# Four transformer layers on one core: the last norm turned by token halves, and another head order in the second attention's first group

## The chip, the cores and the metric

The kernel runs on one core of a Trainium2 chip. The metric is the device time of one launch in microseconds (us). The kernel before was run three times on the chip; a further execution was taken with the hardware profiler.

## What is computed

The input x has 2 batches of 256 tokens and 512 features, 512 tokens in all; the context has 2 batches of 512 tokens. Four layers follow one another. Each one adds an attention block on the normed x to x, and then a feed-forward block on the normed x. Two of these eight blocks matter here.

The second attention (layer 1 of the reference, "l1" in the kernel) has 16 query heads of 96 features and 4 key and value heads, so 4 query heads share one of the latter. Its keys are the 512 context tokens and the 256 tokens of x itself:

```python
hidden = jnp.concatenate([context, latents], axis=1)
q = (latents @ Wq.T).reshape(b, q_len, H, HD)        # H = 16, HD = 96
scores = jnp.einsum('bkgqd,bksd->bkgqs', q, k) * scale
attn = jax.nn.softmax(scores, axis=-1)
```

The last feed-forward block (layer 3) looks at its own normed input before it multiplies: a feature whose largest magnitude over all 512 tokens is above 3 is an outlier.

```python
col_max = jnp.max(jnp.abs(x), axis=tuple(range(x.ndim - 1)))
outlier = col_max > THRESHOLD                        # 3.0
y = _ste_quant_rows(jnp.where(outlier, 0.0, x)) @ _ste_quant_rows(W).T
y = y + jnp.where(outlier, x, 0.0) @ W.T + b
```

So no product with the outliers can start before the largest magnitude of that feature over both token halves is known.

## The kernel before, in words

Every engine has its own hand-ordered program, and semaphores join them. TensorE does all products, nearly all as three passes of a high and a low part (`passes`, L337 to L341). ScalarE (ACT) writes high parts, VectorE (DVE) low parts, GpSimd (POOL) splits the weights, and the queue of SyncE (SP) issues every DMA, one after the other in program order.

**Attention.** The class `Attention` (from L729) works in slots. A group of 4 heads and 2 batches has 16 tiles of 128 queries, one for each slot k; two tiles are a unit (one head of one batch, 256 queries). In slot k TensorE computes the scores of tile k (`scores`, L1190), DVE the row maximum (`largest`, L1306), ACT the exponential; one slot later ACT and DVE write the two fp16 parts of the probabilities (L1258, L1360), and SP issues the DMA that transposes them (`cross_probs`, L1100). The scores go round two banks, so tile k waits for the DVE part of tile k-2 (L1209). At slot 2u+5 TensorE multiplies unit u with the values (`attend`, L1221), which have come through a transposing DMA too (`cross_values`, L1108); ACT and DVE then write its two output planes over the unit's queries (L1298, L1394), which DVE signals by `s_olo`. Projections of the next group's queries, keys and values and of the last group's output are dealt out to the slots by lists (`FIRST`, `MIDDLE`, `LAST`, L587 to L602).

**The packed fourth head of l1.** A head has 96 rows, so the projection makes three tiles of 128 rows: heads 0, 1 and 2 with 32 rows of head 3 below each. Six DMAs, two for each tile, assemble head 3 (`move_queries`, L864, `s_qmove`); in the first group they are issued at slots 1 and 2, between the transposes. For the same reason the output of head 3 is spread back under the three others by six DMAs for each batch (`move_out`, L872), before the output projection: for the first batch at slot 10 of the group, for the second at slot 2 of the next. `move_out` waits for `s_olo`. The order in which the units take the heads is `head` (L833): 0, 1, 3, 2 in all four groups of l1. Head 3 so is the third unit (tiles 4 and 5), and `move_out` waits for three units of its batch.

In l1 the queue of SP also loads rows of the last block's weights, one DMA in each slot from 8 to 39 (`RowMaxima`, L605): DVE takes the row maxima two slots later (L630).

**The last norm.** `Norm` 7 (L399) turns the normed x so that features lie on partitions. DVE adds the last output tile to x, takes the statistics, and waits for the inverse deviation from POOL (L463); the first two token tiles were normed before, so TensorE turns them while the third and fourth are still being made. Each of the four banks holds one block of 128 features with all 512 tokens (L499 to L506), so a bank is full only when the fourth token tile has been turned. Then ACT copies it to `xF` (L2209), DVE takes the largest magnitudes (L2221) and the masks (L2222, L2223), ACT writes the high part of the outliers (L2206) and DVE the low part (L2217), feature block by feature block. TensorE starts the first product (`out_first`, L2240) block by block as the low parts come. ACT and DVE next take the largest magnitude of each token (L2320, L2400), which TensorE turns after the second output tile (L2231). POOL splits the next weights meanwhile (L2178, L2180). Norms 1, 3 and 5 already turn by halves of 256 tokens, with a bank for two feature blocks of one half (L487 to L498).

## Time and profile before

| | |
|---|---|
| runs of the kernel | 1871.99, 1865.81, 1871.82 us; median 1871.82 us |
| the profiled execution, its own time | 1868.25 us |
| its span, first to last instruction | 1866.5 us |
| TensorE busy | 1746.1 us (94% of the span) |
| VectorE busy | 1427.1 us (76%) |
| ScalarE busy | 1048.1 us (56%) |
| GpSimd busy | 886.5 us (47%) |
| mean granted TensorE clock | 0.981 of full speed |

The span leaves 1.75 us of the profiled execution's time outside. All times of the trace are from the span's start. An engine's busy time says how much it had to do; where it waited and for whom stands in the views by waits and in the timelines. PE is the matmul side of TensorE, SPq the DMA queue that SyncE drives. A granted clock of 1.00 in a stretch is the level of 2.4 GHz, 0.50 that of 1.2 GHz.

### The profile page before, as it was taken

How to read it: one execution, taken by the hardware profiler on the slowest of the kernel's cores; microseconds unless marked ns; L12 is line 12 of the kernel's file. 1: busy time of each engine (PE TensorE's matmuls, PEld its weight loads, DVE VectorE, ACT ScalarE, POOL GpSimd, SP SyncE). 2: the span in 40 equal slices, each digit the busy share in tenths (PEclk: the TensorE clock that was granted, in tenths of full speed). 3: DMA queues.
4: the chain of work that ended last, by engine and by line, in shares of the span. 5: the costliest groups of instructions: out<-in, count | busy, mean ns of one | idle time of the engine just before them, and what ended most of it. 6: DMA issues, size and time to landing. Idle time of an engine off the chain costs nothing.

```text
span 1866.5 us, 29004 instructions
## 1 busy us (share of the span) xinstructions
PE 1746.1 (94%) x9916; PEld 1417.3 (76%) x9916; DVE 1427.1 (76%) x3036; ACT 1048.1 (56%) x1999; POOL 886.5 (47%) x863
## 2 busy tenths in 40 slices
PE   6999999999888999979899999999989999998988
PEld 5777777787677788868788888888867778776755
DVE  6877888878777887756777778778864687787898
ACT  5766677667126555632656556556641487776233
POOL 6876776774732222053434444343347541333752
PEclk9999999999999999989999999999999999998998
DMA  5666656566418988761788878979762100120110
GB/s 183 139 115 147 138 117 142 132 116 123 118 29 167 208 194 168 145 132 57 136 164 182 156 161 182 172 159 200 137 142 104 51 15 10 48 90 29 68 45 23
DMA packets 524177, 226.13 MB, mean 121 GB/s; under 512 B 493696, under 2 KB 503168, under 8 KB 516736
## 3 DMA queue, kind: packets, MB, share of 16 engines
q1 hardware_dynamic: 524032, 224.28, 55.6%
q8 instruction: 81, 1.33, 0.3%
q14 instruction: 64, 0.52, 0.1%
HBM read 97.08 MB, written 5.24 MB: 55 GB/s over the span
## 4 chain that ended last, share of the span: by engine, by line
PE 66%; DVE 18%; ACT 5%; DMA 4%; issue 4%; POOL 2%; SPq 2%; DVEq 0%; POOLq 0%; ACTq 0%
PE ps_t L339 9%; PE ps_t L340 8%; PE ps_t L341 8%; PE ps_s L339 7%; PE ps_s L341 7%; PE ps_s L340 7%; PE ps_o L339 3%; PE ps_o L340 3%; PE ps_o L341 3%; PE ps_o L1961 3%; PE ps_t L1992 3%; ACT ps_s L1285 2%; PE ps_s L1947 2%; DVE l_q_lo L1035 2%; DVE l_ab L1360 2%
## 5 line engine op out<-in xcount | busy, mean ns | idle before, releaser
L1285 ACT ACTIVATE ps_s<-ps_s,nmax 128x768 f32<-128x768 f32 (+1 forms) x320 | 252.4, 789 | 326.7 <-DVE nmax L1315 242.5
L1258 ACT ACTIVATE l_ab<-ps_s,rinv 128x768 f16<-128x768 f32 (+1 forms) x320 | 260.6, 814 | 80.6 <-DVE rinv L1370 58.0
L1360 DVE SCALAR_TENSOR_TENSOR l_ab<-ps_s,rinv,l_ab 128x768 f16<-128x768 f32 (+1 forms) x320 | 288.9, 903 | 4.4 <-ACT l_ab L1258 4.0
L1315 DVE TENSOR_REDUCE nmax<-ps_s 128x1 f32<-128x768 f32 x192 | 183.4, 955 | 125.0 <-PE ps_s L341 124.4
L339 PE MATMUL ps_o<-l_pt,l_v 128*128 128x256 f16 (+1 forms) x832 | 231.3, 278 | 14.0 <-DMA l_pt<-l_ab 6.4
L341 PE MATMUL ps_o<-l_pt,l_v 128*128 128x256 f16 (+1 forms) x832 | 230.0, 276 | 0.0
L340 PE MATMUL ps_o<-l_pt,l_v 128*128 128x256 f16 (+1 forms) x832 | 229.9, 276 | 0.0
L339 PE MATMUL ps_s<-l_k_hi,l_q_hi 128*128 128x512 f32 (+3 forms) x512 | 187.0, 365 | 25.6 <-DVE l_ab L1360 20.7
L377 POOL TENSOR_TENSOR wo_hi<-raw_big,one 128x512 fp32r<-128x512 f32 (+2 forms) x100 | 102.8, 1028 | 201.7 <-PE ps_t L341 123.3
L340 PE MATMUL ps_s<-l_k_lo,l_q_hi 128*128 128x512 f32 (+3 forms) x512 | 180.3, 352 | 0.0
L341 PE MATMUL ps_s<-l_k_hi,l_q_lo 128*128 128x512 f32 (+3 forms) x512 | 180.0, 352 | 0.0
L377 POOL TENSOR_TENSOR wq_hi<-raw_big,one 128x512 fp32r<-128x512 f32 (+1 forms) x100 | 102.2, 1022 | 137.2 <-DMA raw_big<-in_l_wq 64.6
L339 PEld LDWEIGHTS ps_s<-l_k_hi,l_q_hi 128*128 128x128 f32 (+1 forms) x512 | 96.9, 189 | 64.7 <-DVE l_ab L1360 33.6
L379 POOL TENSOR_TENSOR wq_lo<-raw_big,wq_hi 128x512 fp32r<-128x512 f32 (+1 forms) x100 | 129.0, 1290 | 7.8
L716 POOL TENSOR_TENSOR w_raw<-w_raw,w_row 128x512 f32<-128x512 f32 x32 | 41.4, 1293 | 188.0 <-DMA w_raw<-in_f_w 188.0
L379 POOL TENSOR_TENSOR wo_lo<-raw_big,wo_hi 128x512 fp32r<-128x512 f32 (+2 forms) x100 | 121.3, 1213 | 7.8
L2100 DVE TENSOR_TENSOR l_pt_lo<-ps_t,l_pt_hi 128x512 fp32r<-128x512 f32 x128 | 88.4, 691 | 46.8 <-ACT l_pt_hi L2034 43.9
L339 PE MATMUL ps_t<-xT_hi,wq_hi 128*128 128x512 f32 (+1 forms) x296 | 117.5, 397 | 4.3 <-DVE xT_lo L2217 3.1
L339 PEld LDWEIGHTS ps_o<-l_pt,l_v 128*128 128x128 f16 (+1 forms) x832 | 87.4, 105 | 43.1 <-issue 29.9
L1312 DVE CUSTOM_DVE_ANT_0 ps_s<-ps_s,l_mask 128x512 f32<-128x512 f32 x128 | 88.6, 692 | 40.8 <-PE ps_s L341 40.6
L340 PE MATMUL ps_t<-xT_lo,wq_hi 128*128 128x512 f32 (+1 forms) x296 | 111.2, 376 | 0.0
L341 PE MATMUL ps_t<-xT_hi,wq_lo 128*128 128x512 f32 (+1 forms) x296 | 110.9, 375 | 0.0
(390 smaller groups left out, 4949.3 us busy)
## 6 DMA issues: line engine op xcount, KB each, us to landing
raw_big<-in_l_wq SPq DMA_DIRECT2D x18, 1024.0 KB, 5.7
raw_big<-in_l_wo SPq DMA_DIRECT2D x18, 1024.0 KB, 6.0
w_raw<-in_f_w SPq DMA_DIRECT2D x32, 256.0 KB, 3.5
raw_big<-in_f_w SPq DMA_DIRECT2D x7, 1024.0 KB, 4.8
raw_kv<-in_l_wkv SPq DMA_DIRECT2D x12, 512.0 KB, 6.6
l_pt<-l_ab SPq DMA_TRANSPOSE x320, 3.7
raw_f<-in_f_w SPq DMA_DIRECT2D x4, 1024.0 KB, 4.7
w_nat<-in_f_w1n SPq DMA_DIRECT2D x16, 256.0 KB, 3.8
```

The source lines that it names most:

```text
L339: pe.matmul(o, a[0], b[0], start=start, stop=False)
L340: pe.matmul(o, a[0], b[1], start=False, stop=False)
L341: return pe.matmul(o, a[1], b[0], start=False, stop=stop)
L377: pool.tensor_tensor(hi, w, one[0:parts, 0:1].to_broadcast([parts, cols]), ALU.mult).then_inc(w_rdy[role], 1)
L379: pool.tensor_tensor(lo, w, hi.bitcast(F32), ALU.subtract).then_inc(w_rdy[role], 1)
L1258: e.activation(sp.ab[:, (k - 1) % 3, 0, :], self.scores_out(k - 1), ACT.Copy, scale=rinv[:, i:i + 1]).then_inc(s_pa, 1)
L1285: e.activation(self.scores_out(k), self.scores_out(k), ACT.Exp, bias=nmax[:, i:i + 1], scale=-1.0 if l.rope else 1.0, accum_out=rsum[:, i: ...
L1312: e.tensor_tensor_reduce(out=o, in0=o, in1=sp.mask[:, 2 * b + qt, :], scale=-1.0, scalar=F32_MAX, op0=ALU.add, op1=ALU.min, accum_out=nmax ...
L1315: e.tensor_reduce(nmax[:, i:i + 1], o, AX.X, ALU.max, negate=True).then_inc(s_max, 1)
L1360: e.scalar_tensor_tensor(out=b, in0=self.scores_out(t), scalar=rinv[:, i:i + 1], in1=a, op0=ALU.mult, op1=ALU.subtract).then_inc(s_pb, 1)
L1961: mm = e.matmul(ps_o[:, 0:SQ], l3v[blk % 2][:, k, g * P:(g + 1) * P], l3pt[u % 2][y][:, k, :], start=g == 0 and k == 0 and y == 0, stop=g ...
L2100: e.tensor_tensor(pt[1], ps_t[p % 2][:, :].rearrange("p (k q) -> p k q", q=P), pt[0].bitcast(F32), ALU.subtract).then_inc(s3["tlo"], 1)
```

## The change

The first part concerns the last norm. TensorE turns it as norms 1, 3 and 5: the first two token tiles fill two banks, each with two feature blocks of 256 tokens, and the last two fill the other two. ACT copies a bank as soon as it is full, so the first half's two before the second half is normed. The new helper `f3_norm_largest` takes the largest magnitudes of one bank (two feature blocks, 256 tokens). DVE calls it for the first half's banks after the statistics and before it norms the second half, and for the second half's afterwards. A small new instruction takes the larger of the two halves' values, and the masks are made for two feature blocks at once. The new tile `q_cm_halves` holds the values of the halves.

The second part concerns l1. In its first group (its first 8 units) the heads come in the order 0, 1, 2, 3; the other groups keep 0, 1, 3, 2. `move_out` of the first group therefore waits for four units of its batch and not for three.

```diff
--- before.py
+++ after.py
@@ -206,6 +206,7 @@
         q_cm = at("q_cm", [P, HT], F32, 61.5625)
         q_mo = at("q_mo", [P, HT], F32, 61.625)
         q_mi = at("q_mi", [P, HT], F32, 61.6875)
+        q_cmh = at("q_cm_halves", [P, 2, DK], F32, 61.84375)
         q_tm = at("q_tm", [P, TT], F32, 61.75)
         q_ts = at("q_ts", [P, TT], F32, 61.78125)
         h = at("h", [P, HT, T], F32, R0)
@@ -428,6 +429,8 @@
                 if self.halves:
                     self.dve_stats(e, link, 1)
                     if self.i == 7:
+                        f3_norm_largest(e, 0)
+                        f3_norm_largest(e, 1)
                         self.dve_scale(e, 1)
                         f3_norm_dve(e, link)
                         return
@@ -484,7 +487,7 @@
                 return self.banks[2 * half + p].rearrange("p (d t) -> p d t", d=2)
 
             def pe(self, e, early=None):
-                if self.halves and self.i != 7:
+                if self.halves:
                     for t in range(TT):
                         half = t // 2
                         e.wait_ge(s_xn, TT * self.i + t + 1)
@@ -493,16 +496,8 @@
                                              xn[:, t, d * P:(d + 1) * P], ident[:, :])
                             if t % 2 and d % 2:
                                 mm.then_inc(g_full, 1)
-                        if t == 1:
+                        if t == 1 and early is not None:
                             early(e)
-                    return
-                if self.halves:
-                    for t in range(TT):
-                        e.wait_ge(s_xn, TT * self.i + t + 1)
-                        for d in range(DK):
-                            mm = e.transpose(self.banks[d][:, t * P:(t + 1) * P], xn[:, t, d * P:(d + 1) * P], ident[:, :])
-                            if t == TT - 1:
-                                mm.then_inc(g_full, 1)
                     return
                 e.wait_ge(s_xn, TT * (self.i + 1))
                 if self.i == 0:
@@ -832,7 +827,7 @@
 
             def head(self, u):
 
-                return (0, 1, 3, 2)[u % HG] if self.l.packed else u % HG
+                return (0, 1, 3, 2)[u % HG] if self.l.packed and u >= UNITS else u % HG
 
             def o_planes(self, u, hd):
                 hh, b = self.head(u), u // HG % B
@@ -873,7 +868,7 @@
 
                 cols = slice(b * SQ, (b + 1) * SQ)
                 e.wait_ge(s_qmove, 96 * (g + 1))
-                e.wait_ge(s_olo, self.c.unit + g * UNITS + b * HG + 3)
+                e.wait_ge(s_olo, self.c.unit + g * UNITS + b * HG + (3 if g else 4))
                 for a in self.s.q[g % 2]:
                     for t in range(3):
                         e.dma_start(a[96:P, t, cols].bitcast(F32), a[32 * t:32 * t + 32, 3, cols].bitcast(F32)).then_inc(s_omove[b], 16)
@@ -1190,7 +1185,7 @@
                 def scores(k):
                     g, i = k // TILES, k % TILES
                     u, qt = i // 2, i % 2
-                    b, hh = u // HG, self.head(u)
+                    b, hh = u // HG, self.head(g * UNITS + u)
                     if b == 0 and qt == 0:
                         if hh < l.qt:
                             self.operand_ready(e, self.find["q", g, hh, False])
@@ -2202,28 +2197,40 @@
 
         def f3_norm_act(e):
             def hi(d):
-                e.wait_ge(s4["x_mask"], 2 * d + 2)
+                e.wait_ge(s4["x_mask"], 2 * (d // 2) + 2)
                 e.activation(xT[0][:, d, :], xF[:, d, :], ACT.Copy, scale=q_mo[:, d:d + 1]).then_inc(g_hi, 1)
+            for n in range(4):
+                half, p = n // 2, n % 2
+                e.wait_ge(g_full, cf.g - 4 + n + 1)
+                e.activation(xF[:, 2 * p:2 * p + 2, half * SQ:(half + 1) * SQ], norms[7].half_bank(half, p), ACT.Copy)\
+                    .then_inc(s4["x_kept"], 1)
             for d in range(DK):
-                e.wait_ge(g_full, cf.g - 4 + d + 1)
-                e.activation(xF[:, d, :], last_norm_banks[d], ACT.Copy).then_inc(s4["x_kept"], 1)
-                if d:
-                    hi(d - 1)
-            hi(DK - 1)
+                hi(d)
+
+        def f3_norm_largest(e, n):
+            half, p = n // 2, n % 2
+            e.wait_ge(s4["x_kept"], n + 1)
+            return e.tensor_reduce(q_cmh[:, half, 2 * p:2 * p + 2], xF[:, 2 * p:2 * p + 2, half * SQ:(half + 1) * SQ], AX.X, ALU.max,
+                                   apply_absolute_value=True)
 
         def f3_norm_dve(e, link):
             def lo(d):
                 e.wait_ge(g_hi, START["ln7"].hi + d + 1)
                 e.scalar_tensor_tensor(out=xT[1][:, d, :], in0=xF[:, d, :], scalar=q_mo[:, d:d + 1],
                                        in1=xT[0][:, d, :].bitcast(F32), op0=ALU.mult, op1=ALU.subtract).then_inc(g_free, 1)
-            for d in range(DK):
-                e.wait_ge(s4["x_kept"], d + 1)
-                link(e.tensor_reduce(q_cm[:, d:d + 1], xF[:, d, :], AX.X, ALU.max, apply_absolute_value=True))
-                e.tensor_scalar(q_mo[:, d:d + 1], q_cm[:, d:d + 1], 3.0, None, ALU.is_gt).then_inc(s4["x_mask"], 1)
-                e.tensor_scalar(q_mi[:, d:d + 1], q_cm[:, d:d + 1], 3.0, None, ALU.is_le).then_inc(s4["x_mask"], 1)
-                if d:
-                    lo(d - 1)
-            lo(DK - 1)
+
+            def masks(p):
+                two = slice(2 * p, 2 * p + 2)
+                link(e.tensor_tensor(q_cm[:, two], q_cmh[:, 0, two], q_cmh[:, 1, two], ALU.max))
+                e.tensor_scalar(q_mo[:, two], q_cm[:, two], 3.0, None, ALU.is_gt).then_inc(s4["x_mask"], 1)
+                e.tensor_scalar(q_mi[:, two], q_cm[:, two], 3.0, None, ALU.is_le).then_inc(s4["x_mask"], 1)
+            link(f3_norm_largest(e, 2))
+            masks(0)
+            link(f3_norm_largest(e, 3))
+            lo(0)
+            masks(1)
+            for d in range(1, DK):
+                lo(d)
 
         def f3_pe(e):
             def turn_largest(o):
```

## Rows read from the trace of the kernel before

**Rows 1.** The page: busy time of the engines, share of the span.
```profile
PE 1746.1 (94%) x9916; PEld 1417.3 (76%) x9916; DVE 1427.1 (76%) x3036; ACT 1048.1 (56%) x1999; POOL 886.5 (47%) x863
```
**Rows 2.** The page: the chain that ended last, shares of the span.
```profile
PE 66%; DVE 18%; ACT 5%; DMA 4%; issue 4%; POOL 2%; SPq 2%; DVEq 0%; POOLq 0%; ACTq 0%
```
**Rows 3.** Timeline of TensorE, first group of l1: start, us, instruction, idle before, releaser.
```profile
565.82 0.49 PE L339 MATMUL ps_s<-l_k_hi,l_q_hi 96*128 96x512 f32 x1 [3.87 <-DMA l_q_lo<-l_q_lo]
...
571.47 0.41 PE L339 MATMUL ps_o<-l_pt,l_v 128*96 128x256 f16 x1
...
574.35 0.48 PE L339 MATMUL ps_s<-l_k_hi,l_q_hi 96*128 96x512 f32 x1
```
**Rows 4.** Timeline of VectorE in the same stretch.
```profile
562.47 1.00 DVE L1360 SCALAR_TENSOR_TENSOR l_ab<-ps_s,rinv,l_ab 128x768 f16<-128x768 f32 x1
...
567.44 0.96 DVE L1315 TENSOR_REDUCE nmax<-ps_s 128x1 f32<-128x768 f32 x1 [2.57 <-PE ps_s L341]
...
575.69 0.96 DVE L1315 TENSOR_REDUCE nmax<-ps_s 128x1 f32<-128x768 f32 x1
```
**Rows 5.** Busy time by stretch: PE, PEld, DVE, ACT, POOL; then granted clock, DMA.
```profile
562.00:566.00 4.00, 0.18 (x1) 0.18 (x2) 2.70 (x5) 2.74 (x5) 0.00 (x0) 1.00 0.81 160
566.00:570.00 4.00, 3.30 (x14) 2.74 (x15) 2.39 (x5) 1.15 (x3) 0.00 (x0) 0.59 0.84 157
...
624.00:628.00 4.00, 2.82 (x15) 2.10 (x14) 3.21 (x7) 1.51 (x3) 0.00 (x0) 1.00 1.06 163
```
**Rows 6.** Timeline of SP's queue, slots 4 to 17 of l1.
```profile
565.82 1.83 SPq L1113 DMA_TRANSPOSE l_v<-l_vab  x1
...
594.25 0.85 SPq L622 DMA_DIRECT2D w_nat<-in_f_w1n  x1
595.20 1.80 SPq L879 DMA_DIRECT2D l_q_hi<-l_q_hi  x3
...
598.99 1.44 SPq L1105 DMA_TRANSPOSE l_pt<-l_ab  x1
...
625.48 0.58 SPq L622 DMA_DIRECT2D w_nat<-in_f_w1n  x1
```
**Rows 7.** The line of `cross_values` (L1113) from 560 to 570 us: its landing.
```profile
DMA to landing us min/median/max: 3.8/3.8/3.8
```
**Rows 8.** Timeline of VectorE, slots 11 to 18 of l1.
```profile
597.21 0.47 DVE L1394 SCALAR_TENSOR_TENSOR l_q_lo<-ps_o,v_out_scale,l_q_hi 96x256 fp32r<-96x256 f32 x1
...
605.83 0.67 DVE L630 TENSOR_REDUCE q_sw<-w_nat 128x1 f32<-128x512 f32 x1
...
619.33 0.69 DVE L630 TENSOR_REDUCE q_sw<-w_nat 128x1 f32<-128x512 f32 x1 [0.52 <-DMA w_nat<-in_f_w1n]
...
628.89 0.69 DVE L630 TENSOR_REDUCE q_sw<-w_nat 128x1 f32<-128x512 f32 x1 [1.50 <-DMA w_nat<-in_f_w1n]
```
**Rows 9.** The first `attend` of the third attention: timeline of TensorE.
```profile
902.03 0.39 PE L339 MATMUL ps_o<-l_pt,l_v 128*128 128x256 f16 x1 [2.76 <-DMA l_v<-l_vab]
```
**Rows 10.** Busy time by stretch after it, columns as in Rows 5.
```profile
902.00:906.00 4.00, 3.96 (x19) 2.85 (x20) 0.01 (x1) 0.00 (x0) 2.14 (x2) 0.50 0.71 151
```
**Rows 11.** Timeline of all engines in the last norm.
```profile
1715.73 1.00 DVE L418 TENSOR_SCALAR xn<-x,mv,rstd 128x512 f32<-128x512 f32 x2 [0.81 <-POOL rstd L463]
...
1717.25 1.08 ACT L2209 ACTIVATE xF<-ps_s 128x512 f32<-128x512 f32 x2 [10.76 <-PE ps_s L503]
...
1717.88 0.69 DVE L2221 TENSOR_REDUCE q_cm<-xF 128x1 f32<-128x512 f32 x1 [1.15 <-ACT xF L2209]
...
1720.88 0.76 PE L339 MATMUL ps_t<-xT_hi,wq_hi 128*128 128x512 f32 x1 [3.12 <-DVE xT_lo L2217]
...
1725.67 0.79 PE L339 MATMUL ps_t<-xT_hi,wq_hi 128*128 128x512 f32 x1
...
1730.26 0.66 PE L2231 MATMUL ps_s<-ident,q_amx 128*128 128x128 f32 x4 [0.20 <-DVE q_amx L2400]
```
**Rows 12.** The line of the low parts (L2217): duration in ns, least, median, largest.
```profile
L2217 DVE SCALAR_TENSOR_TENSOR xT_lo<-xF,q_mo,xT_hi x4: 741/1030/1562, 1719.6 to 1724.1; 128x512 fp32r<-128x512 f32 x4
```

## The prediction

> **What bounds the kernel now.** I read the page first: TensorE is busy for 94% of the span [rows 1] and has 66% of the chain that ended last, VectorE 18% [rows 2]. So a gain must shorten a stretch in which TensorE waits or runs at a low clock, and must not be given back by a later wait. The change touches two such stretches, which I read in the timelines.
>
> *Start of the second attention (l1).* The scores of tile 4, the first that need the assembled head 3, start at 565.82 after 3.87 us of idle time, released by the last of the moving DMAs [rows 3]. Their other condition, the probabilities of tile 2, was met at 562.47 + 1.00 = 563.5 [rows 4]. So head 3 costs 2.3 us there. Behind it the clock falls: TensorE has 0.18 us of work in 562 to 566, and from 566 to 570 the granted clock is 0.59, against 1.00 before [rows 5]. It is the level of 1.2 GHz for most of the time up to about 573.5; the first unit's products with the values, 571.47 to 574.35, run mostly in it, and so last 2.9 us [rows 3].
>
> *Slots 10 to 16 of the same group.* The queue of SP issues without a gap from the row DMA at 594.25 to the one at 625.48 (31 issues from the first up to the last; none begins over 0.12 us after the end of the one ahead) [rows 6]. Its last one releases VectorE at 628.89 after a wait of 1.50 us, an earlier one at 619.33 after 0.52 us [rows 8]. TensorE, full before, has 2.82 of 4 us in 624 to 628 [rows 5]. So at 628.89 it is SP's queue that sets the time of all engines; what they gain before it is lost there unless SP starts earlier too.
>
> *The last norm.* VectorE waits 0.81 us for the inverse deviation, norms the second half at 1715.73, ACT copies from 1717.25, the first maximum starts at 1717.88 and the first product at 1720.88; its last block starts at 1725.67 [rows 11]. The next thing that TensorE waits for is the turned token maxima, at 1730.26 with 0.20 us of wait [rows 11].
>
> **Part 1, the head order.** Nothing is added or removed: the same 12 moving DMAs, the same matmuls. Moved are the uses of head 3 (tiles 4, 5 to tiles 6, 7) and the condition of `move_out`.
>
> *The ramp.* Tile 4 starts at 563.5 in place of 565.8. Tile 5 then follows at about 566.9, a period of 3.4 us as between the tiles ahead. Its scores end at 568.3. Now the first unit's product with the values is next, and that needs the transposed values: issued at 565.82 behind the same DMAs as before, landed 3.8 us later, at 569.6 [rows 6, 7]. It was no wait before; now it is one of 1.3 us or a little more. If the clock is full, the product takes some 2 us in place of 2.9 (estimate: the part up to 573.5 halved), and tile 6 starts at 572.0 in place of 574.35 [rows 3]: a gain of 2.3 us. If the clock falls at this new wait, the product takes 3.9 us, tile 6 starts at 573.8 and its own scores take 1.2 us longer, so the maximum of tile 6, at 575.69 before [rows 4], comes 0.6 us later. For that stands the same spot of the third attention, which has no moved head: there the first product with the values waits 2.76 us for just this transfer [rows 9], and the clock of the 4 us behind is 0.50 [rows 10]. Ends: +2.3 and -0.6 us. I take 1.3: the new wait is half as long as that one, and work lies on both sides of it.
>
> *The hold at slot 10.* `move_out` of the first batch waited for unit 2; now it waits for unit 3, whose low part is written at 597.21 + 0.47 = 597.7 [rows 8]. SP was free for it at 595.1 [rows 6]. Behind it in the queue stand the transpose of tile 10 (598.99) and everything to 625.48 [rows 6]. Relative to the engines SP stops for 2.6 us. If the engines are d earlier, the queue starts 2.6 - d later than before, and since it runs without a gap, so does the issue at 625.48 and the release at 628.89. The rows between take part of the loss ahead of time (the row of 605.83 had about 1.7 us to spare, that of 619.33 none [rows 8]), but not twice. So part 1 is worth 2.6 - d, not -d: with d = 1.3 it costs 1.3 us; ends 0.3 and 3.2. The second batch's `move_out` waits for unit 7, which is done about when SP comes to it: nothing. The DMAs of slot 13 and 15, queries and weights of the next groups, come late with the queue; they had slots to spare.
>
> **Part 2, the norm.** The two maxima of the first half are 0.69 us each [rows 11], 1.38 us in a wait of 0.81: the second half is normed 0.57 us later. POOL's power runs beside them, so I put its cost at nothing; if they slowed it, that would cost its excess in full. A bank is full after the second block, not the first: 0.1 us. So VectorE's first maximum behind it starts at 1718.55. One maximum 0.69, the larger of two and the masks 0.45 (estimate from the small instructions around, 0.15 each), one high part 0.7 on ACT with the second maximum beside it, one low part 1.1 to 1721.5; masks 0.45; three low parts at 1.03 to 1.1 [rows 12] to 1725.2. Before, four maxima and four pairs of masks stood between the low parts, to 1725.6. So VectorE gains 0.4 us; with all three at 0.74 or at 1.56 [rows 12] it would be a gain of 1.4 or a loss of 1.0. TensorE starts at 1721.5 in place of 1720.88, but without gaps: twelve passes of 512 columns at 1.2 GHz are 5.1 us (estimate), to 1726.6, before 1727.1. Half of that half microsecond counts, since the clock returns no earlier, and the 0.20 us of wait may go. I take -0.2 us; ends -0.7 and +0.9. The early ACT copies cost nothing: ACT idles there. POOL's weight split begins 0.57 us later and is wanted some 9 us after its end.
>
> **Sum.** 1.3 - 0.2 = +1.1 us. On the profiled execution's 1868.25 us that is 1869.4. The median of the runs shown is 1871.82, 3.6 us above that execution, with one run at 1865.81; I take the middle of execution and median, 1870.0, as the base: **1871.1 us**.
>
> **The rivals.** *Faster: the ramp's gain is kept.* SP's queue turns out elastic: its transposes took 1.4 to 2.9 us each, and after a pause they may take the shorter time. Then d = 2.3 stays and the norm's 0.2 to 0.7 comes on top: 1867.3 us. Against it stands the release at 628.89, straight from the queue.
>
> *Slower: the clock falls at the first product with the values, and the hold is paid in full.* Place: 568 to 577 us. Price: 0.6 us at tile 6 and 2.6 at the hold, less 0.2: +3.0, 1873.0 us. It decides once the wait for the values grows from the 1.3 us of my sum towards the 2.76 of [rows 9]; a transfer slower by 1 us, as tile 3's transpose is now issued right behind it, would do.
>
> *Slower in the norm: the low parts come one after another.* They took up to 1.56 us, the longest without a maximum in front [rows 12]. If each is stopped by a weight split of POOL, three of them end at 1726.6, TensorE starts its last block 0.9 us late, and the norm costs 0.7 instead of gaining 0.2: 1872.0 us. The Trainium skill's page "SBUF — State Buffer", section "SBUF: two separate sides", says that a VectorE instruction with two SBUF inputs and a GpSimd one that reads SBUF hold a shared port as an exclusive lock, and "Who interferes with whom" there says that a reduction never contends; by that rule the reductions leave the interval between the low parts and only contending work is left, as in this rival. The spread of [rows 12] agrees with a lock, but its median of 1.03 does not show every one stopped.
>
> *The change doesn't do what it says:* the maxima of the first half do not fit in the wait (1.38 against 0.81 us), which my sum has; if they also come late, because ACT's copies do, up to 0.6 us more.
>
> **How the numbers follow.** Forecast 0.45; gain kept 0.17; clock and hold 0.20; norm's low parts 0.12; the rest 0.06. Base and changes: the best is -2.3 - 0.7 on the lowest run, 1863; the worst +3.2 + 0.9 on 1872, and a longer half-clock stretch of up to 2 us, 1878. Range 1863 to 1878. A change of 0.5% is 9.3 us, about what a measurement of this kernel can tell from none; no case reaches it. I leave 0.03 for faster and 0.04 for slower, 0.93 for the same.
>
> **What would show it.** TensorE's wait for the moved query should be gone and one for the transposed values stand before the first product with the values; `move_out` should start at the low part of unit 3 with SP idle ahead of it; VectorE should wait longer in total for the weight rows up to slot 18. In the norm the wait for the inverse deviation is gone, the first product starts about 0.6 us later and its last block 0.4 us earlier. I am wrong if SP's queue has gaps between slots 11 and 16, if the stretch from the start of l1 to the end of its first group is over 2 us shorter, or if the norm changes by over 1 us.

## The result, and the profile after

The changed kernel takes 1874.76 us (median of 17 runs, 1867.77 to 1880.21), the kernel before, run beside it, 1867.72 us (17 runs, 1859.52 to 1874.33). The ratio is 1.0038, with a 95% interval of 1.0026 to 1.0051: 7.1 us slower, 4.9 to 9.5 by the interval. A later measurement of both gave 1.0016 (1.0000 to 1.0032), that is 3.0 us. The first says slower, by 0.3 to 0.5%; the second's interval reaches down to no difference. A value of about 5 us lies in both intervals. The profiled execution took 1878.34 us with a span of 1876.5. Two of the 12 executions of the run with the heads alone, below, were slow (2621.55 and 6008.47 us) and are left out of its ratio, though not of its median.

**The page after.** TensorE's busy time is 6.1 us up on [rows 1], VectorE's 5.3; VectorE's share of the chain that ended last went from 18% [rows 2] to 20%.

```profile
PE 1752.2 (93%) x9908; PEld 1425.0 (76%) x9916; DVE 1432.4 (76%) x3034; ACT 1048.9 (56%) x1999; POOL 885.3 (47%) x863
...
PE 66%; DVE 20%; ACT 5%; issue 3%; DMA 3%; POOL 2%; SPq 1%; DVEq 0%; POOLq 0%; ACTq 0%
```

**The last norm after.** VectorE's timeline: start, us, instruction, idle time before it and what ended it. It answers to [rows 11, 12].

```profile
1722.14 0.17 DVE L414 TENSOR_SCALAR veps<-mv 128x2 f32<-128x2 f32 x1
1722.21 1.27 DVE L2213 TENSOR_REDUCE q_cm_halves<-xF 128x2 f32<-128x512 f32 x2
1723.40 0.99 DVE L419 TENSOR_SCALAR xn<-x,mv,rstd 128x512 f32<-128x512 f32 x2
1726.20 0.69 DVE L2213 TENSOR_REDUCE q_cm_halves<-xF 128x2 f32<-128x512 f32 x1 [1.80 <-ACT xF L2205]
1726.92 0.95 DVE L2224 TENSOR_TENSOR q_cm<-q_cm_halves 128x2 f32<-128x2 f32 x1
1727.91 0.17 DVE L2225 TENSOR_SCALAR q_mo<-q_cm 128x2 f32<-128x2 f32 x1
1727.98 1.24 DVE L2226 TENSOR_SCALAR q_mi<-q_cm 128x2 f32<-128x2 f32 x1
1729.14 0.67 DVE L2213 TENSOR_REDUCE q_cm_halves<-xF 128x2 f32<-128x512 f32 x1
1730.08 0.75 DVE L2219 SCALAR_TENSOR_TENSOR xT_lo<-xF,q_mo,xT_hi 128x512 fp32r<-128x512 f32 x1 [0.27 <-ACT xT_hi L2201]
1730.75 1.23 DVE L2224 TENSOR_TENSOR q_cm<-q_cm_halves 128x2 f32<-128x2 f32 x1
1732.02 0.97 DVE L2225 TENSOR_SCALAR q_mo<-q_cm 128x2 f32<-128x2 f32 x1
1732.90 0.16 DVE L2226 TENSOR_SCALAR q_mi<-q_cm 128x2 f32<-128x2 f32 x1
1732.97 3.09 DVE L2219 SCALAR_TENSOR_TENSOR xT_lo<-xF,q_mo,xT_hi 128x512 fp32r<-128x512 f32 x3
```

Two numbers per partition are compared in each of the small instructions, and four of six take 0.95 to 1.24 us where the prediction had 0.15 each. Beside them GpSimd splits the second weight chunk without a gap (its timeline):

```profile
1724.48 1.04 POOL L2173 TENSOR_TENSOR wo_hi<-raw_big,one 128x512 fp32r<-128x512 f32 x1 [1.39 <-DVE xn L419]
1725.59 1.26 POOL L2175 TENSOR_TENSOR wo_lo<-raw_big,wo_hi 128x512 fp32r<-128x512 f32 x1
1726.82 1.04 POOL L2173 TENSOR_TENSOR wo_hi<-raw_big,one 128x512 fp32r<-128x512 f32 x1
1727.94 1.26 POOL L2175 TENSOR_TENSOR wo_lo<-raw_big,wo_hi 128x512 fp32r<-128x512 f32 x1
1729.16 1.04 POOL L2173 TENSOR_TENSOR wo_hi<-raw_big,one 128x512 fp32r<-128x512 f32 x1
```

The slow comparisons end where a split ends: the one from 1727.98 ends at 1729.22, the split at 1729.20. TensorE waits for what comes of them (its timeline), and its clock is at the lower level of 1.2 GHz meanwhile (busy time by stretch, columns as in [rows 5]):

```profile
1730.98 0.76 PE L340 MATMUL ps_t<-xT_hi,wq_hi 128*128 128x512 f32 x1 [5.02 <-DVE xT_lo L2219]
1733.76 0.79 PE L340 MATMUL ps_t<-xT_hi,wq_hi 128*128 128x512 f32 x1 [1.17 <-DVE xT_lo L2219]
```

```profile
1726.00:1731.00 5.00, 0.02 (x1) 0.05 (x1) 4.46 (x7) 1.99 (x4) 4.84 (x5) 0.50 0.70 262
1731.00:1741.00 10.00, 8.79 (x21) 5.99 (x22) 8.28 (x12) 4.47 (x7) 3.77 (x3) 0.54 0.29 105
```

To compare kernels whose stages start at different times I count from veps, the instruction that adds 1e-5 to the second half's variance (1714.75 in before, 1722.14 here). The first product starts at 8.84 instead of 6.13, the copy of the fourth output tile by ACT at 25.89 instead of 21.69. From there on the tiles keep their distance of 4.2 us to the end of the 16 tiles (66.76 against 62.56). The count from veps to the end of the span says what the norm's part is worth to the whole kernel: in the five profiles of all runs that keep the norm of before it is 150.2 to 151.7 us (mean 150.9), in the four with the norm of the change 154.2 to 154.5 (mean 154.3), so 3.4 us.

**The start of l1 after.** TensorE's timeline, SP's queue, and TensorE again near slot 15; they answer to [rows 3], [rows 6] and [rows 8].

```profile
570.83 0.45 PE L340 MATMUL ps_o<-l_pt,l_v 128*96 128x256 f16 x1 [2.25 <-DMA l_v<-l_vab]
...
621.16 0.28 PE L340 MATMUL ps_o<-l_pt,l_v 128*96 128x256 f16 x1 [0.75 <-issue]
```

```profile
595.09 0.83 SPq L617 DMA_DIRECT2D w_nat<-in_f_w1n  x1
598.75 1.80 SPq L874 DMA_DIRECT2D l_q_hi<-l_q_hi  x3
600.59 1.85 SPq L874 DMA_DIRECT2D l_q_lo<-l_q_lo  x3
602.54 2.42 SPq L1100 DMA_TRANSPOSE l_pt<-l_ab  x1
```

```profile
570.00:574.00 4.00, 3.17 (x15) 3.02 (x16) 0.82 (x3) 0.60 (x2) 0.00 (x0) 0.50 1.06 198
```

The wait for the moved head is gone, a wait of 2.25 us for the transposed values has taken its place, and the clock in the 4 us behind it is 0.50. SP's queue stands idle for 2.8 us (595.92 to 598.75) before the moves, and the transpose of slot 10 behind them is issued at 602.54 instead of 598.99.

### The profile page after: what moved, and what is told of

Same layout as the page of the kernel before. It is cut to its first block, busy times and chain, and to the rows that moved or that the text cites. A ratio compares the mean times of both kernels' runs of the same rounds, so it can differ in the third digit from the quotient of the medians.

```text
span 1876.5 us, 28995 instructions
## 1 busy us (share of the span) xinstructions
PE 1752.2 (93%) x9908; PEld 1425.0 (76%) x9916; DVE 1432.4 (76%) x3034; ACT 1048.9 (56%) x1999; POOL 885.3 (47%) x863
## 4 chain that ended last, share of the span: by engine, by line
PE 66%; DVE 20%; ACT 5%; issue 3%; DMA 3%; POOL 2%; SPq 1%; DVEq 0%; POOLq 0%; ACTq 0%
PE ps_t L340 9%; PE ps_t L341 8%; PE ps_t L342 8%; PE ps_s L340 7%; PE ps_s L342 7%; PE ps_s L341 7%; PE ps_o L340 3%; PE ps_o L1956 3%; PE ps_o L341 3%; PE ps_o L342 3%; PE ps_t L1987 3%; ACT ps_s L1280 2%; PE ps_s L1942 2%; DVE nmax L1310 2%; DVE l_q_lo L1030 2%
```

## The experiments

Each run has its own time and that of before, taken in turns on the same chip; the difference is worked out from the ratio of the two (1.0021 is 3.9 us). The median of before was 1866.85 to 1868.46 us in these measurements.

| run | median us, runs | ratio to before (95%) | first high part | last low part ends | fourth tile |
|---|---|---|---|---|---|
| before | 1867.72, 17 | 1 | 4.10 | 10.86 | 21.69 |
| the change | 1874.76, 17 | 1.0038 (1.0026 to 1.0051) | 7.12 | 13.92 | 25.89 |
| the change again | 1870.81, 12 | 1.0016 (1.0000 to 1.0032) | 7.12 | 13.92 | 25.94 |
| norm alone | 1872.64, 12 | 1.0021 (1.0004 to 1.0037) | 5.85 | 13.76 | 25.23 |
| heads alone | 1871.47, 12 | 1.0022 (1.0002 to 1.0041) | 4.09 | 10.87 | 21.68 |
| norm, fused on one column | 1867.85, 12 | 1.0007 (0.9987 to 1.0028) | 5.16 | 12.20 | 22.30 |
| norm, splits behind the masks | 1870.83, 12 | 1.0011 (0.9988 to 1.0035) | 5.26 | 10.97 | 25.06 |
| norm, one column, tensor_tensor kept | 1871.75, 10 | 1.0023 (1.0007 to 1.0039) | 5.02 | 13.75 | 25.24 |
| norm, fused, one maximum ahead | 1866.23, 12 | 0.9995 (0.9979 to 1.0010) | 4.88 | 11.91 | 22.01 |

The last three columns are us behind veps, from the profile of each.

**The two parts by themselves.** The first run leaves out the head order, the second the norm's part.

```diff
-                return (0, 1, 3, 2)[u % HG] if self.l.packed and u >= UNITS else u % HG
+                return (0, 1, 3, 2)[u % HG] if self.l.packed else u % HG
-                e.wait_ge(s_olo, self.c.unit + g * UNITS + b * HG + (3 if g else 4))
+                e.wait_ge(s_olo, self.c.unit + g * UNITS + b * HG + 3)
```

> Only the last norm's part of the change; heads in the order of before. Theory (both parts cost, the norm's by its small VectorE instructions standing in GpSimd's weight splits): first high part about 7.1 us behind veps (4.1 in before), first product of the final stage about 8.8 us behind veps (6.1), time +3 to +4.5 us over before. Rival A (the head order makes all of the 7 us): 0 +- 1 us. Rival B (the norm makes all, the heads' loss is absorbed by the end): +6 to +7.5 us.

> Only the head order with its later moves; the last norm as before. Theory: the second attention's cross part ends about 3 us later (the wait for v, the clock at its lower level behind it, the SP queue held about 3 us), time +2 to +4 us. Rival A (the head order makes all): +6 to +7.5 us. Rival B (absorbed later on): 0 +- 1 us.

Measured +3.9 (0.7 to 6.9) and +4.1 us (0.4 to 7.7). Either part costs, if only just beyond its interval, and the sum of 8 agrees with the 7.1 of the whole. The intervals are too wide to put a rival with all the cost in one part out by the times alone; the positions can: the norm's part alone moves the fourth tile by 3.5 us, the heads alone by nothing (21.68). The first high part came at 5.85 and the first product at 7.76, earlier than the 7.1 and 8.8 expected from the change's profile: there the third copy by ACT starts 3.43 us behind veps, here 2.79, so some 0.6 us of the change's 4.2 are not its small instructions.

**What stops the small instructions.** In the first of three runs no two-column instruction and no tensor_tensor is left among the masks: the other half's maximum comes in as the scalar.

```diff
-                link(e.tensor_tensor(q_cm[:, two], q_cmh[:, 0, two], q_cmh[:, 1, two], ALU.max))
-                e.tensor_scalar(q_mo[:, two], q_cm[:, two], 3.0, None, ALU.is_gt).then_inc(s4["x_mask"], 1)
+                for d in (2 * p, 2 * p + 1):
+                    one_d = slice(d, d + 1)
+                    e.tensor_scalar(q_mo[:, one_d], q_cmh[:, 0, one_d], q_cmh[:, 1, one_d], 3.0, ALU.max, ALU.is_gt).then_inc(s4["x_mask"], 1)
```

> The norm's part alone, but the larger of the two halves and the comparison are one instruction on one column (128x1) with the other half as its scalar, so no two-column instruction and no tensor_tensor is left among the masks. Theory (two-column and two-input instructions are stopped by GpSimd's splits, one-column ones are not, as in before): each small one 0.14 to 0.20 us, first high part 4.2 to 4.8 us behind veps, time -1 to +1 us against before and 2.5 to 4 us under the norm's part alone. Rival (the order of the turns and the copies costs, not the small instructions): still +3 us or more.

```profile
1718.84 0.21 DVE L2225 TENSOR_SCALAR q_mo<-q_cm_halves 128x1 f32<-128x1 f32 x1
1718.97 0.20 DVE L2226 TENSOR_SCALAR q_mi<-q_cm_halves 128x1 f32<-128x1 f32 x1
...
1720.04 1.61 DVE L2219 SCALAR_TENSOR_TENSOR xT_lo<-xF,q_mo,xT_hi 128x512 fp32r<-128x512 f32 x1
```

None of the eight is stopped (0.20 to 0.22 us), the low part of 128x512 beside them is (1.61 us). The fourth tile is back from 25.2 to 22.3, and from veps to the end of the span it is 151.1 us instead of 154.1. The time is +1.3 us (-2.4 to +5.2), which by itself is not told apart from the norm's part alone. The first high part, at 5.16, missed the expected 4.2 to 4.8. The second run keeps the change's own instructions and holds GpSimd back until the masks stand:

```diff
                     e.wait_ge(s3["job_full"], L3_JOBS)
+                    e.wait_ge(s4["x_mask"], 4)
```

> The norm's part alone as the change has it, but GpSimd's splits of the second weight chunk wait until the last mask stands. Theory (GpSimd's instructions stop the small ones): two-column masks and the larger of the halves 0.15 to 0.25 us each without GpSimd beside them, first high part under 5 us behind veps, first product about 6 us behind veps, time -1 to +1 us. Rival (they are slow of themselves, about 1 us each): no change to the norm's part alone, +3 us.

```profile
1719.12 0.16 DVE L2225 TENSOR_TENSOR q_cm<-q_cm_halves 128x2 f32<-128x2 f32 x1
1719.32 0.17 DVE L2226 TENSOR_SCALAR q_mo<-q_cm 128x2 f32<-128x2 f32 x1
1719.39 0.17 DVE L2227 TENSOR_SCALAR q_mi<-q_cm 128x2 f32<-128x2 f32 x1
```

The same six instructions take 0.15 to 0.17 us without GpSimd beside them, so they are not slow of themselves. The expected positions were missed all the same: the first high part came at 5.26 us (under 5 expected), the first product at 6.98 (about 6), and the first tile at 12.08 is no gain, since the five profiles with the norm of before have it at 11.98 to 12.67. And the splits now fell on the four tensor_tensor of the tokens' largest magnitude (5.54 us in all), for which TensorE waits behind the second tile: third tile at 22.33 against 18.97, time +2.1 us (-2.2 to +6.5), where -1 to +1 was expected. The third run separates two inputs from two columns:

```diff
+                    link(e.tensor_tensor(q_cm[:, one_d], q_cmh[:, 0, one_d], q_cmh[:, 1, one_d], ALU.max))
+                    e.tensor_scalar(q_mo[:, one_d], q_cm[:, one_d], 3.0, None, ALU.is_gt).then_inc(s4["x_mask"], 1)
```

> The norm's part alone with everything small on one column, but the larger of the halves by tensor_tensor (two inputs in SBUF) and the comparisons by themselves, to part the two kinds of instruction. If both kinds are stopped by GpSimd's splits for their own reasons (two inputs; two columns): the four tensor_tensor of 128x1 take 0.5 to 1.3 us each where GpSimd runs, the eight comparisons 0.14 to 0.17 us, time +2 to +4 us. If only two-column instructions are stopped: all 0.15 to 0.2 us, time +0 to +1.5 us. If GpSimd stops whatever comes: comparisons of 0.5 us and more among them.

```profile
1716.42 0.60 DVE L2225 TENSOR_TENSOR q_cm<-q_cm_halves 128x1 f32<-128x1 f32 x1
1717.05 0.15 DVE L2226 TENSOR_SCALAR q_mo<-q_cm 128x1 f32<-128x1 f32 x1
1717.12 0.14 DVE L2227 TENSOR_SCALAR q_mi<-q_cm 128x1 f32<-128x1 f32 x1
1717.18 0.83 DVE L2225 TENSOR_TENSOR q_cm<-q_cm_halves 128x1 f32<-128x1 f32 x1
```

The first of the three outcomes, its time too (+4.3 us, 1.3 to 7.3): the four tensor_tensor of one number per partition take 0.60 to 1.18 us, the comparisons of one column 0.14 to 0.15. With the norm alone, two of the four comparisons of two columns took 0.97 and 1.25 us. So there are two separate reasons to be stopped: two inputs in SBUF, down to one number per partition, and a comparison of two columns. The Trainium skill's page "SBUF — State Buffer", section "Who interferes with whom", names both: two SBUF inputs against a GpSimd instruction that reads SBUF, and a mode that reads one tensor through both ports. The Trainium skill's page "VectorE: DVE Perf Modes", section "Mode 2×_2P — use both read ports for one tensor", wants for that mode that the outermost dimension larger than one is even, or odd and equal in source and destination. These runs agree with both pages: 128x2 has such a dimension and was stopped (up to 1.25 us), 128x1 has none and was not (0.14 to 0.15).

**One maximum ahead of the rows.** As the fused kernel, with the second maximum of the first half behind the normalised rows.

```diff
-                        f3_norm_largest(e, 1)
                         self.dve_scale(e, 1)
+                        f3_norm_largest(e, 1)
```

> The norm's part with one-column comparisons, and only one of the first half's two maxima ahead of the normalised rows, the other behind them, where VectorE idled 1.8 us. Theory (two maxima of 1.27 us do not fit into the wait of 0.81 us; one of 0.69 us does): xn 0.98 us behind veps as in before instead of 1.26, first product and the tiles of the final stage 0.3 us earlier than with one-column comparisons alone, time -1 to +0.5 us against before. Rival: another term (the copies' order, the clock) sets the start, tiles as with one-column comparisons alone within 0.1 us, +0.5 us.

The rows start 0.98 us behind veps (1.26 before that edit), every tile comes 0.28 us earlier than with the fused kernel. As expected; the time of -0.9 us (-3.9 to +1.9) against before is no measurable gain.

**The moves of the fourth head.** Three runs have SP's queue in another way. In the first two the heads stand in the order 0 to 3 as in the change, the norm as in before, and the first batch's moves are issued at slot 12 or 11 instead of 10; the third is before with nothing but the longer wait.

```diff
-                if s == 10:
+                if s == (10 if g else 12):
```

> The head order alone (last norm as before), with the first batch's moves of the fourth head issued two slots later, so that the SP queue finds the fourth unit done. Theory (the order's cost is the hold of the SP queue and the clock at the wait for v): no idle time of the queue between slots 9 and 10's transposes, the transposes of slot 10 on about 3 us earlier than with the head order alone, the cross part's slots 20 on at +1 to +2 us instead of +3, time +0 to +2.5 us over before, 1.5 to 3 us under the head order alone. Rival (the hold is hidden by the rounding's slack, all the cost is the clock at v): as the head order alone, +3 to +4 us.

> The head order alone, the first batch's moves of the fourth head issued one slot later (two slots later they only stood in front of the weight loads and the transpose of slot 13 was as late as with the hold). Theory (what costs is that the SP queue's run of moves and weight loads, which lasts until slot 15, is begun 3 us late): the moves find the fourth unit done and fill idle time of the queue, the transposes of slots 13 to 15 less than 1.5 us later than in before (counted from the stage's start), no wait of TensorE for a probability transpose near slot 15, time +0 to +2 us, what the clock at v leaves. Rival (the hold isn't what costs): as the head order alone, +3 to +4 us.

> Before with one edit: the moves of the first group wait for the fourth unit of their batch instead of the third; heads in the order 0, 1, 3, 2, last norm as before. Theory: the SP queue is held 2.5 to 3.5 us at slot 10, the slots from 20 on are 1.5 to 3 us later, time +1.5 to +3 us. Rival (the hold is hidden): 0 +- 1 us, slots from 20 on within 0.5 us of before.

Measured +3.0 (-0.2 to +6.2), +2.1 (-1.1 to +5.2) and +5.6 us (+2.6 to +8.8). The intervals of the first two hold the expected times and their rivals' alike; the third lies above the +1.5 to +3 expected. SP's queue in the run with slot 11, and its waits from 590 to 610 us (in total, times, longest):

```profile
595.50 0.90 SPq L622 DMA_DIRECT2D w_nat<-in_f_w1n  x1
597.65 1.42 SPq L1105 DMA_TRANSPOSE l_pt<-l_ab  x1
599.12 0.88 SPq L622 DMA_DIRECT2D w_nat<-in_f_w1n  x1
600.10 1.80 SPq L879 DMA_DIRECT2D l_q_hi<-l_q_hi  x3
601.94 2.69 SPq L879 DMA_DIRECT2D l_q_lo<-l_q_lo  x3
604.73 1.47 SPq L1105 DMA_TRANSPOSE l_pt<-l_ab  x1
```

```profile
SPq L1105 <- DVE l_ab L1360: 3.0, 3, 1.2
```

No idle time is left ahead of the moves there, but the queue is not busy throughout: with the moves out of the way it comes to the transposes before their probabilities are written, and waits for them three times, 3.0 us in total (596.40 to 597.65 is one). Before has no wait of the queue from 590 to 608 us; the change has 3.1 us from 590 to 610, nearly all ahead of the moves. Counted in every profile from 39.5 to 63 us behind slot 0, the queue waits 0.3 to 2.1 us for probabilities or for the moves' unit where the moves stand as in before, 2.3 to 3.0 with slot 11, 3.6 with slot 12, and 2.8 to 3.5 with the hold. Single executions wander by some us with the stretches of low clock, so I read a shorter distance, in the same way in every profile: between the row maxima (nmax) of two slots of l1, by the kernel's own slot numbers (slot 0 at 550.84 in before).

| kernels | profiles | slot 0 to 6 | 16 to 24 | 0 to 38 |
|---|---|---|---|---|
| order 0, 1, 3, 2, moves as in before | 10 | 25.5 (23.7 to 26.8) | 36.8 (35.3 to 37.9) | 162.1 (159.8 to 164.0) |
| order 0 to 3, moves held at slot 10 | 4 | 25.0 (24.0 to 25.6) | 38.9 (38.3 to 39.7) | 163.9 (162.8 to 164.7) |
| order 0 to 3, moves at slot 11 | 3 | 24.9 (23.9 to 25.6) | 39.6 (39.0 to 40.9) | 164.7 (164.3 to 165.0) |
| order 0 to 3, moves at slot 12 | 1 | 24.2 | 39.7 | 163.7 |
| hold alone | 1 | 24.7 | 38.8 | 163.9 |

(Mean, least and largest.) The order gains about 0.5 us on the mean by slot 6, less than the profiles differ among themselves. The stretch of slots 16 to 24 separates the groups: not one of the nine kernels with later moves is as short as the longest of the ten others. So the hold costs about 2.1 us there and 1.8 by the end of the cross part, where the ranges overlap, and the run with the hold alone shows the same by itself (its time, +5.6, is more than its slots account for; the rest was not found).

The clock enters this table. In slots 16 to 24 the granted clock is 1.00 throughout in seven of the ten profiles (mean 36.4 us), in the hold alone and in three of the four held ones (38.7); it has a stretch of the lower level, mean 0.955 to 0.958, in the three others of the ten (37.7), in the change (39.7) and in all with slot 11 or 12. At like clock the hold costs 2.2 and 2.0 us, slot 11 costs 1.3, 1.4 and 3.2, and slot 12 costs 2.0.

Moving the moves so did not give the time back, but it is no proof against the idle time as the cause either, since the queue idles in these runs too. What goes along with the cost in all nineteen profiles is how late the queue is behind the moves. Its last load of the next group's weights (raw_kv) ends 29.0 to 29.8 us behind the maximum of slot 8 in the ten, 30.5 to 31.2 with slot 11, 31.6 with slot 12, and 31.4 to 32.1 with the hold. No run has the new order and a queue that is on time, so whether the lateness is all of the cost is not shown.

**Both parts mended, and each within the whole.** The first run has fused columns, one maximum ahead and slot 11; the others are the change again, with the norm mended alone, and with slot 11 alone.

> The whole change with both parts mended: one-column comparisons, one maximum ahead of the normalised rows, moves of the fourth head at slot 11. Theory: the 7 us of the change go down to the sum of the mended parts, -1 to +2 us against before. Rival (the change's cost lies elsewhere, in the clock behind v or in the turning by halves itself): +4 us or more.

> The changed kernel as it is, on the chip and in the rounds of the three runs below, as their measure. Expected by every theory: +5 to +9 us over before, the first of the larger-of-halves and comparison instructions stopped to about 1 us each, fourth output tile 25 to 26 us behind veps.

> The changed kernel with the norm's part alone mended (one-column comparisons, one maximum ahead of the rows). Theory (each part makes 3 to 4 us of its own): 3 to 5 us under the changed kernel, +2 to +4 us over before. Rival (with the head order in place the norm's mending brings nothing, the cost being the clock's phase): within 1 us of the changed kernel.

> The changed kernel with the head order's part alone mended (moves of the fourth head at slot 11). Theory (hold of the SP queue 1 to 3 us): 1 to 3 us under the changed kernel, +3.5 to +6 us over before. Rival (the hold is hidden in the whole): as the changed kernel.

Both mended: 1868.99 us, +0.9 us (-3.0 to +4.9). The change again: +3.0 us, under the +5 to +9 expected. Norm mended alone: 1866.64 us, ratio 1.0000 (0.9983 to 1.0017), its fourth tile at 21.62; +2 to +4 us was expected. Slot 11 alone: 1872.88 us, ratio 1.0028 (1.0011 to 1.0046), fourth tile 25.76; 1 to 3 us less than the change was expected, and it is 2.2 us more. So the norm's mending gives back 3.0 us beside the change again, and the moves at slot 11 give nothing, as the table of slots says too. The four profiles with the fused comparisons and GpSimd beside them end 150.1 to 151.1 us behind veps, as with the norm of before (150.2 to 151.7); with the tensor_tensor kept it is 154.2, as with the change. That the norm's mending leaves no cost at all, with the hold still in place, is not explained; the interval (-3.2 to +3.2 us) has room for the 1.8 of the slots.

**GpSimd out of the way.** In before, too, low parts are stopped (up to 1.56 us [rows 12]). Four runs, on top of the fused norm, hold the splits of the second chunk back: behind the largest magnitude (the first line of the diff); behind the low parts (g_free in place of it), with the largest turned behind the third tile; the same with the spread of the scales' rows behind the sixth tile; the same with the first whole-number tile behind the ninth tile. TensorE takes that chunk piece by piece.

```diff
+                    e.wait_ge(s4["largest"], 1)
...
+                    if j % 4 == 0:
+                        e.wait_ge(w_rdy[role], 8 * ((cf.q, cf.o)[chunk % 2] + chunk // 2) + 2 * d + 2)
...
-        INT_BEHIND = {7: 0, 9: 1, 11: 2, 12: 3, 13: 4, 14: 5}
+        INT_BEHIND = {8: 0, 9: 1, 11: 2, 12: 3, 13: 4, 14: 5}
```

> As the run with one maximum ahead of the rows, and GpSimd's splits of the second weight chunk wait until the magnitudes' largest stands, while TensorE takes that chunk's pieces one by one. Theory (what is left of the norm's cost is GpSimd beside VectorE): low parts 0.75 us each (1.14 to 1.5 with GpSimd beside them), their end 8.5 to 9.2 us behind veps (10.9 in before), third output tile 1.5 to 2.5 us earlier than in before, fifth tile on within 1 us of that, time -1 to -3 us against before. Rival (the second chunk becomes late): fifth tile later than in before, time +0 to +2 us.

> As the run with GpSimd's splits held back, but only until the last norm's low parts stand, and the magnitudes' largest is turned behind the third output tile instead of the second. Theory (the splits behind the largest came 3 us too late for the fifth tile): low parts still 0.75 us each, splits about 3 us earlier, fifth output tile 25 to 26.5 us behind veps (26.2 in before, 28.3 with the splits behind the largest), time -2 to 0 us against before. Rival (the turned largest becomes late and holds the fourth or fifth tile): fifth tile 27 us or later, time +0 to +2 us.

> As the run with GpSimd's splits behind the low parts, and the spread of the token scales moved behind the sixth output tile (behind the fourth TensorE waited 4.3 us for them). Theory (GpSimd beside VectorE is what the last norm's start costs, also in before): first four tiles 2 to 3 us earlier than in before as in that run, and now kept at the seventh tile and on; time -3 to -1 us against before. Rival (what is won is handed to the next wait, for the whole-number first tile): tiles from the ninth on at or behind before's, time 0 +- 1.5 us.

> As the run with the rows' spread behind the sixth tile, and the first whole-number tile behind the ninth output tile instead of the eighth (behind the eighth TensorE waited 3.4 us for its operand). Theory (the 2.5 us that VectorE wins without GpSimd beside it can be kept if no consumer waits): ninth output tile 34.6 to 35.5 us behind veps (38.0 in before with the whole-number tile ahead of it, about 37 without), tenth tile 1.5 to 2.5 us earlier than in before, time -3 to -0.5 us. Rival (VectorE's chain, not TensorE, sets the rest of the stage): last output tiles within 0.5 us of before's or later, time 0 +- 1.5 us.

| run | median us | ratio (95%) | lows end | tiles 4, 5, 7, 9, 16 |
|---|---|---|---|---|
| before | 1867.72 | 1 | 10.86 | 21.69, 26.21, 31.65, 38.01, 62.56 |
| behind the largest | 1871.33 | 1.0011 (0.9995 to 1.0026) | 8.94 | 20.55, 28.32, 33.76, 40.12, 64.67 |
| behind the lows | 1873.05 | 1.0032 (1.0014 to 1.0050) | 8.39 | 19.17, 31.18, 36.63, 42.99, 67.54 |
| and rows later | 1870.40 | 1.0014 (0.9996 to 1.0031) | 8.30 | 19.20, 21.91, 29.15, 38.87, 63.42 |
| and whole-number tile later | 1867.80 | 0.9988 (0.9969 to 1.0007) | 8.94 | 20.51, 23.23, 30.47, 35.91, 62.60 |

Without GpSimd beside them the low parts end 1.9 to 2.6 us earlier than in before, and the fourth tile comes up to 2.5 us earlier. In each of the first three runs the next consumer takes it back. Behind the low parts the splits fall on the four tensor_tensor of the tokens' largest magnitude, which take 5.9 us in the last three runs (2.87 behind the largest). TensorE's timelines of the last three runs:

```profile
1738.36 2.08 PE L2245 MATMUL ps_s<-diag,ones 128*128 128x128 f32 x8 [4.33 <-DVE diagr L2379]
```

```profile
1746.34 0.81 PE L2269 MATMUL ps_t<-xq,q_w 128*128 128x512 bf16 x3 [3.42 <-issue]
```

```profile
1749.83 0.81 PE L2269 MATMUL ps_t<-xq,q_w 128*128 128x512 bf16 x3 [0.74 <-issue]
...
1772.01 1.04 PE L2269 MATMUL ps_o<-xq,q_w 128*128 128x512 bf16 x4 [0.36 <-DVE q_t L2429]
...
1785.37 1.32 PE L2269 MATMUL ps_t<-xq,q_w 128*128 128x512 bf16 x4 [2.07 <-DVE q_t L2429]
```

The rivals of these runs hit: the fifth tile late in the first (28.32), the rows late in the second, whose +6.0 us lie beyond its rival's 0 to +2 too, the whole-number operand late in the third. In the last one TensorE waits no longer than 0.74 us behind its first product up to the sixteenth tile. The ninth tile is 2.1 us ahead of before, in part because the first whole-number tile now stands behind it, and the tenth 0.5; the sixteenth stands where it stood (62.60 against 62.56). So the rival that VectorE's chain sets the rest hit for the tiles. But the tiles are not the end: behind them TensorE waits for VectorE's q_t in either kernel, at 67.8 and 73.8 us behind veps in before (1.45 and 2.17 us of wait), at 72.15 here (1785.37, 2.07 us), and the span ends 149.1 us behind veps, 1.1 us less than in the shortest profile with the norm of before. That is one profile; the 1867.80 us is the best ratio of all, -2.2 us (-5.8 to +1.3), and not told apart from before. No version was found that beats before measurably.

## Why the prediction was wrong

The forecast was +1.1 us on a base of 1870.0. Before measured 1867.7 beside the change, so the base was 2.3 us high; the time of 1874.8 lay in the range, but the difference was 6 us more than forecast by the first measurement and 1.9 more by the second.

- **Part 1, the ramp:** predicted a gain of 1.3 us between -0.6 and +2.3. The wait for the values appeared where it was said, at 2.25 us instead of 1.3, and the clock fell to 0.50 behind it, so this execution has the rival's case: the maximum of slot 6 is 0.6 us later (25.48 against 24.85 from slot 0). The sum had the transposed values issued as early as in before; counted from slot 0 they were issued 1.1 us later (16.05 against 14.98), behind a transpose of 2.63 us. Over 8 profiles with the new order and 11 with the old one the gain is 0.5 us on the mean, not 1.3.
- **Part 1, the hold:** predicted 2.6 us less what the engines gain, with the moves right behind unit 3's low part and SP idle ahead. Both are in the trace (idle 2.8 us). With the 0.5 us of the ramp that makes 2.1, and the held profiles are 2.1 us longer in slots 16 to 24 and 1.8 by the end of the cross part. That VectorE would wait longer in total for the weight rows up to slot 18 came true: 3.0 us in this row of the waits after (588 to 632 us) against 2.0 in before; the row that the prediction gave 1.7 us to spare now makes it wait 1.43, at 608.34. TensorE has 0.75 us of idle time ahead of a product with the values (shown above); the view puts it down to issue, and what it waited for is not shown.

```profile
DVE q_sw L625 <- DMA w_nat<-in_f_w1n: 3.0, 3, 1.4
```

- **Part 1 in sum:** +1.3 predicted (0.3 to 3.2), +1.8 by the slots. The size was right, and the mechanism, a queue that is late behind the moves, is what the profiles show; that the idle time is all of it is not shown.
- **Part 2, the maxima in the wait:** rows 0.57 us later predicted; measured 1.26 - 0.98 = 0.28, since the two maxima take 1.27 us together and not 1.38, and the first starts 0.07 us behind the start of veps, while the sum has it start in the wait behind it.
- **Part 2, "the larger of two and the masks 0.45": this is the step that failed.** The three took 0.95 + 0.17 + 1.24, from 1726.92 to 1729.14 with the next instruction's start, 2.2 us; the second set 2.2 us again (1730.75 to 1732.97). Twice 1.8 us are 3.5 us on the path of the first product and of the last block. The estimate came from the one-column comparisons of before, 0.15 each beside the same splits, and did not see that the change makes them two columns wide and adds an instruction with two inputs. With that undone, the first high part starts 5.16 us behind veps, and 4.88 with one maximum ahead of the rows, where the prediction's own sum has 4.94 (1718.55 + 0.69 + 0.45 less 1714.75).
- **Part 2, the low parts:** predicted to end at 10.5 us behind veps (1725.2). They ended at 13.92, 3.1 later than in before.
- **Part 2 in sum:** -0.2 predicted, ends -0.7 and +0.9; measured +3.5 to +4.3 by the fourth tile and +3.4 on the mean by the end of the span, in the four profiles with the norm of the change, and +3.9 us as a time. The ends were too narrow because both were made from the durations of the low parts alone.
- **The rivals:** "low parts one after another" put the lock on the right engine pair, and cited the rule, but looked only at the 128x512 instructions; 0.7 us was its price. The same rule applied to each new instruction of the change would have marked the small ones as well, and four of them, stopped for about the length of a split (1.04 or 1.26 us), make the 3.5; four of six were. "Clock and hold" came true in the execution after as to its events; its 3.2 us for part 1 are above the 1.2 that this profile's slots 0 to 38 are longer than those of before (164.65 against 163.49), and above the 2.6 against the mean of the ten.

With 1.8 for part 1 and 3.4 for part 2 the sum is 5.2 us, inside both measured intervals (4.9 to 9.5, and 0 to 6.0). That the time of 1874.8 lay in the range was luck: the range was wide for the base and the clock, and neither end had the step that failed.

## What to carry to other kernels

When a change puts small VectorE instructions on the path, price each by what runs on GpSimd beside it and not by its size: 128x1 with one tensor input stayed at 0.14 to 0.22 us, 128x2 or two SBUF inputs cost up to 1.25 us, about the length of a GpSimd split (1.26). Fusing the larger-of-two into the comparison, on one column at a time, took two more instructions and 3 us less (fourth tile 22.3 against 25.2). Time won at the start of a stage has to be followed to the end of the kernel: 2.5 us won at the fourth tile were gone by the ninth (38.87 against 38.01), and in the last run, whose sixteenth tile stood where it stood in before, the span still ended 1.1 us or more earlier by this one profile. And when a DMA queue no longer idles at one place, look at the others: with the six moves one slot later it waited 3.0 us ahead of the transposes instead.

## What the runs showed that was not expected

- A VectorE instruction that handles two numbers per partition can last 1.25 us: the four stopped ones took 0.95 to 1.24 us in the change and 0.15 to 0.17 us with GpSimd held back; a tensor_tensor of a single number per partition took 0.60 to 1.18 us.
- A comparison with its scalar taken from a column in SBUF (128x1) was never stopped: 32 of them in four profiles with GpSimd busy, at 0.20 to 0.22 us.
- TensorE's clock turned the same work around: the fourth tile comes 21.62 us behind veps where the first pair of turns took 0.44 us and the first high part began at 4.23, and 22.01 where the pair took 0.69 us and the high part began at 4.88, with the same instructions.
- Six moves of 3.7 us in SP's queue cost the slots behind them 1.3 to 3.2 us at like clock, whether the queue idled ahead of them or, with the moves later, ahead of the transposes of slots 9 to 11.
